# The penalty of each score as a 17th lane of the query-key products, laid by ScalarE, in a windowed attention on one core

## The reference

```python
q = _ln(silu(x @ Wq).reshape(B, L, H, D), q_g, q_b)      # H = 16 heads of D = 16
k = _ln(silu(x @ Wkv)[..., :C].reshape(B, L, H, D), ...)
wp = silu(x @ Wwin + bwin)
width = sigmoid(wp[..., :H]) * 8 + 0.5
sharp = sigmoid(wp[..., H:]) * 9.5 + 0.5
rel = abs(arange(17) - 8)
scores = stack([einsum('blhd,blhd->blh', q, k_pad[:, w:w+L]) for w in range(17)]) * D ** -0.5
soft_mask = sigmoid((width[..., None] - rel) * sharp[..., None])
attn = softmax(scores - (1.0 - soft_mask) * 1e4, axis=-1)
out = sum(attn[..., w] * v_pad[:, w:w+L] for w in range(17))
x1 = layernorm(x + silu(out @ Wout))
```

## Time and profile before

| | |
|---|---|
| median of 3 runs | 1184.05 us (1183.74 to 1184.78) |
| profiled execution | 1187.74 us, of which the span is 1185.5 us |
| mean granted TensorE clock | 0.927 of full |
| busy share of the span | PE 81%, DVE 70%, ACT 39%, POOL 60% |
| first stage | about 0 to 110 us |
| window stage | about 110 to 500 us |
| cross attention and routing | about 505 to 730 us |
| experts, then the last norm | about 730 to 1145 us, then to the end |

### The profile page before, as it was taken

The page is one execution under the profiler, slowest core; times in us unless marked ns, Lnnn a source line. Parts: engine busy times, 40 slices in busy tenths (PEclk is TensorE's granted clock), DMA queues, the critical chain, the costliest instruction groups (busy, mean ns, idle before and its releaser), DMA issues.

```text
span 1185.5 us, 25126 instructions
## 1 busy us (share of the span) xinstructions
PE 960.9 (81%) x8135; PEld 774.8 (65%) x8136; DVE 825.9 (70%) x1264; ACT 461.7 (39%) x1055; POOL 712.9 (60%) x464
## 2 busy tenths in 40 slices
PE   7983089998989989678788249999999999999940
PEld 4541088888879979656566237777777777777720
DVE  4899999999999998138888764444444444444425
ACT  3676224444444444325656223222222222222215
POOL 3575599999999999200000055666666666666522
PEclk9998589999999999879999569999999999999985
DMA  3262012112211221478674402222222222222236
GB/s 102 72 120 54 22 41 67 53 58 67 66 56 54 67 66 45 168 256 273 193 236 160 164 28 37 47 41 47 42 46 41 45 44 44 44 45 44 27 80 226
DMA packets 70136, 100.46 MB, mean 85 GB/s; under 512 B 9312, under 2 KB 51872, under 8 KB 69152
## 3 DMA queue, kind: packets, MB, share of 16 engines
q1 hardware_dynamic: 52816, 76.86, 20.8%
q0 software_dynamic: 16128, 18.93, 10.1%
q10 hardware_dynamic: 1152, 4.19, 0.9%
HBM read 73.96 MB, written 26.38 MB: 85 GB/s over the span
## 4 chain that ended last, share of the span: by engine, by line
PE 44%; DVE 28%; issue 15%; DMA 5%; POOL 3%; ACT 3%; DVEq 0%; SPq 0%; ACTq 0%; POOLq 0%
PE psum L757 16%; DVE mid L1392 11%; PE psum L765 10%; PE psum L767 5%; PE psum L616 3%; PE psum L685 2%; DMA sum_dram<-arena,mid 2%; DVE psum L1399 2%; PE psum L596 2%; DVE arena L1529 1%; PE psum L749 1%; PE psum L659 1%; ACT arena L1082 1%; PE psum L599 1%; DMA out<-arena 1%
## 5 line engine op out<-in xcount | busy, mean ns | idle before, releaser
L616 PE MATMUL psum<-consts,mid 128*128 128x128 f32 x2176 | 255.5, 279 | 58.4 <-POOL mid L1155 58.4
L616 PEld LDWEIGHTS psum<-consts,mid 128*128 128x128 f32 x2176 | 251.9, 195 | 66.6 <-issue 48.2
L757 PE MATMUL psum<-arena 128*128 128x128 f16 x3456 | 291.2, 221 | 4.6 <-issue 2.7
L757 PEld LDWEIGHTS psum<-arena 128*128 x3456 | 243.4, 98 | 76.2 <-issue 9.5
L1155 POOL TENSOR_TENSOR mid<-arena 128x2304 f32<-128x2304 f32 (+1 forms) x62 | 251.1, 4072 | 10.0 <-POOL arena L1146 7.0
L765 PE MATMUL psum<-arena 128*128 x576 | 218.1, 380 | 5.3 <-DVE arena L1681 1.2
L1233 POOL DMA_INDIRECT sum_dram<-arena,mid x72 | 142.0, 1972 | 46.5 <-issue 24.3
L1690 DVE SCALAR_TENSOR_TENSOR arena<-psum,arena 128x256 f32<-128x256 f32 x72 | 34.8, 484 | 189.8 <-ACT arena L1054 121.4
L767 PE MATMUL psum<-arena 128*128 x576 | 157.0, 273 | 0.0
L1054 ACT ACTIVATE arena<-psum,arena 128x256 f32<-128x256 f32 x72 | 34.1, 473 | 301.5 <-PE psum L767 301.5
L1392 DVE TENSOR_TENSOR mid<-psum,arena 128x4352 f32<-128x4352 f32 x32 | 149.9, 4683 | 0.6 <-issue 0.4
(11 more groups left out here) (194 smaller groups left out, 1443.3 us busy)
## 6 DMA issues: line engine op xcount, KB each, us to landing
arena<-w_t SPq DMA_DIRECT2D x64, 256.0 KB, 2.8
arena<-w_t SPq DMA_DIRECT2D x16, 1024.0 KB, 10.4
arena<-x SPq DMA_DIRECT2D x32, 128.0 KB, 2.1
arena<-x_dram SPq DMA_DIRECT2D x8, 512.0 KB, 5.5
arena<-ctx_t SPq DMA_DIRECT2D x8, 512.0 KB, 6.4
arena<-ctx SPq DMA_DIRECT2D x8, 512.0 KB, 6.9
x_dram<-mid SPq DMA_DIRECT2D x8, 512.0 KB, 3.3
arena<-sum_dram SPq DMA_DIRECT2D x8, 512.0 KB, 4.9
```

Of the source, the lines that this page charges most:

```text
L616: last = nc.tensor.matmul(psum[:, u, c * P:(c + 1) * P], products[half][:, w, c * P:(c + 1) * P], ident, start=(a + w == 0 and c == 0), st ...
L757: last = nc.tensor.matmul(dst, block_of(w, e, 0, c * F + j * P, P), x[:, u, c * P:(c + 1) * P], start=(k == 0 and c == 0), stop=(k == 2 an ...
```

## The change

The products get a 17th lane: `qk_prod` becomes 17 places by 16 heads by 17 lanes. DVE's multiplication writes lanes 0 to 15. ACT writes lane 16 with the penalty, by two activations (Copy with a scale) that read `gate`: 144 and 128 elements, each written 17 elements apart. DVE's sum then reads 4624 elements and writes the penalised scores straight into `score`, in SBUF; `raw` and the two SCALAR_TENSOR_TENSOR instructions go. The sum waits for `penalties_laid`, and ACT lays the penalties of step t at the head of its `window(t)`, before it waits for `score_ready` of t. For t = 0 they are laid earlier, between the square root of the last heads and the second gates, and DVE's sum of step 0 comes after `last_gates`.

To make room, `reach` (no longer read) leaves the constants, and the 128x128 matrix of ones becomes one column read with stride 0 by the two matmuls that use it. The buffers that lay behind `qk_prod` start 272 elements later. ACT's loop is cut at step 24, where the place of `gate` wraps round.

```diff
+LANES = D + 1
+QK = K * H * LANES
...
-        mid = sb("mid", [P, 2 * K * E])
+        mid = sb("mid", [P, QK + K * E])
...
-        ones_pp = sb("ones_pp", [P, P])
+        ones_col = sb("ones_col", [P, 1])
+        ones_pp = ones_col[:, :].to_broadcast([P, P])
...
-        qk_prod = mid[:, 0:K * E]
+        qk_prod = carve(mid, 0, K, H, LANES)
...
@@ ScalarE
-            def window(t, u, i, more=True):
+            def lay_penalties(t, gate_at):
+
+                if past(t, 1):
+                    act.wait_ge(qk_summed, t)
+                gates = row(gate, t + gate_at).rearrange("p a h r -> p r (a h)")
+                lane = qk_prod[:, :, :, D]
+                nc.scalar.activation(lane[:, R:, :], gates, ACT.Copy, scale=-PENALTY / SCALE).then_inc(penalties_laid, 1)
+                nc.scalar.activation(lane[:, R - 1::-1, :], gates[:, 1:, :], ACT.Copy,
+                                     scale=-PENALTY / SCALE).then_inc(penalties_laid, 1)
+
+            def window(t, u, i, gate_at, more=True):
+                if not isinstance(t, int) or t:
+                    lay_penalties(t, gate_at)
                 act.wait_ge(score_ready, t + 1)
                 nc.scalar.activation(score[:, u, :], score[:, u, :], ACT.Exp, scale=SCALE).then_inc(exp_done, 1)
...
             head_roots(GROUPS - 1)
+            act.wait_ge(gate_done, 1)
+            lay_penalties(0, GROUP)
             gates(1)
...
@@ VectorE
+            def sum_products(t, u):
+
+                dve.wait_ge(qk_multiplied, t + 1)
+                dve.wait_ge(penalties_laid, 2 * t + 2)
+                if past(t, 2):
+                    dve.wait_ge(prob_made, t - 1)
+                nc.vector.tensor_reduce(score[:, u, :].rearrange("p (h w) -> p w h", w=K), qk_prod, op=ALU.add,
+                                        axis=AX.X).then_inc(qk_summed, 1)
...
-                nc.vector.tensor_tensor(qk_prod[:, :].rearrange("p (w c) -> p w c", c=E), queries,
-                                        k_all[:, bass.ds(t, K), :], ALU.mult).then_inc(qk_multiplied, 1)
+                nc.vector.tensor_tensor(qk_prod[:, :, :, 0:D], queries.rearrange("p w (h d) -> p w h d", d=D),
+                                        k_all[:, bass.ds(t, K), :].rearrange("p w (h d) -> p w h d", d=D),
+                                        ALU.mult).then_inc(qk_multiplied, 1)
                 if isinstance(t, int) and t == 0:
                     last_heads()
                 if past(t, 1):
                     sum_up(t - 1, 1 - u)
-                dve.wait_ge(qk_multiplied, t + 1)
-                nc.vector.tensor_reduce(raw.rearrange("p (h w) -> p w h", w=K),
-                                        qk_prod[:, :].rearrange("p (w h d) -> p w h d", h=H, d=D), op=ALU.add, axis=AX.X).then_inc(qk_summed, 1)
+                if not (isinstance(t, int) and t == 0):
+                    sum_products(t, u)
                 if past(t, 1):
                     invert(t - 1, 1 - u)
                 if isinstance(t, int) and t == 0:
                     last_gates()
-                    dve.wait_ge(gate_done, 1)
+                    sum_products(0, 0)
...
-                nc.vector.scalar_tensor_tensor(by_head[:, :, R:], gates, -PENALTY / SCALE, raw_by_head[:, :, R:],
-                                               ALU.mult, ALU.add).then_inc(penalised, 1)
-                nc.vector.scalar_tensor_tensor(by_head[:, :, R - 1::-1], gates[:, :, 1:], -PENALTY / SCALE,
-                                               raw_by_head[:, :, R - 1::-1], ALU.mult, ALU.add).then_inc(penalised, 1)
-                dve.wait_ge(penalised, 2 * t + 2)
```

More of the change, by code:

```diff
@@ L46 @@
 MASKED = 1e10
-LOW = 10856
+LOW = 10824
 N_EXP, TOP, F = 8, 2, 1024
@@ L59 @@
 AT_IDENT = 0
-AT_REACH = AT_IDENT + P
-AT_MASK = AT_REACH + K
+AT_MASK = AT_IDENT + P
 AT_BELOW = AT_MASK + P
@@ L76, in host_consts @@
         i == j,
-        wide(np.abs(np.arange(K) - R)),
         np.where(j > i, -MASKED, 0.0),
@@ L171, in decoder_layer @@
         ident = consts[:, AT_IDENT:AT_IDENT + P]
-        reach = consts[:, AT_REACH:AT_REACH + K]
-        ones_pp = sb("ones_pp", [P, P])
+        ones_col = sb("ones_col", [P, 1])
+        ones_pp = ones_col[:, :].to_broadcast([P, P])
         minus_half = sb("minus_half", [P, 2 * H])
@@ L249, in decoder_layer @@
         w_exp = carve(mid, scale_at + 8, 2).bitcast(I32)
-        assert scale_at + 10 <= 2 * K * E
+        assert scale_at + 10 <= QK + K * E
         gate_col = next_low("experts", 4, 1)
@@ L272, in decoder_layer @@
         v_all = carve(big, (CHUNK + ROWS) * E, ROWS, E)
-        qk_prod = mid[:, 0:K * E]
-        av_prod = [carve(mid, K * E, W0, E), carve(mid, (K + W0) * E, K - W0, E)]
+        qk_prod = carve(mid, 0, K, H, LANES)
+        av_prod = [carve(mid, QK, W0, E), carve(mid, QK + W0 * E, K - W0, E)]
         av_last = [carve(mid, 0, W0, E), carve(mid, W0 * E, K - W0, E)]
         x_step = carve(mid, 0, 2, X_QUAD, C, P)
[L278 to L281, removed]
+        act_qk = carve(mid, QK, 2, 2 * E)
+        cen_qk = carve(mid, QK + 4 * E, 2, 2 * E)
+        sq_qk = carve(mid, QK + 8 * E, 2, 2 * E)
+        head_r = carve(mid, QK + 12 * E, GROUP, 2 * H)
         gate = next_low("window", CHUNK, H, R + 1)
@@ L388, in decoder_layer @@
         qk_summed = sem("qk_summed")
-        penalised = sem("penalised")
+        penalties_laid = sem("penalties_laid")
         q_beside = sem("q_beside")
@@ L643, in _ @@
             pe.wait_ge(w_summed, 1)
-            nc.tensor.matmul(psum[:, 0, 0:2], ones_pp[:, :], w_sum[:, :], start=True, stop=True).then_inc(w_total, 1)
+            nc.tensor.matmul(psum[:, 0, 0:2], ones_pp, w_sum[:, :], start=True, stop=True).then_inc(w_total, 1)
             def transpose_x1(u, c):
@@ L725, in _ @@
                              picked.rearrange("p t n -> p (t n)"), start=True, stop=True)
-            nc.tensor.matmul(psum[:, 1, 0:TILES * N_EXP], ones_pp[:, :],
+            nc.tensor.matmul(psum[:, 1, 0:TILES * N_EXP], ones_pp,
                              picked.rearrange("p t n -> p (t n)"), start=True, stop=True).then_inc(counted, 1)
@@ L937, in _, with windows @@
             head_roots(GROUPS - 1)
+            act.wait_ge(gate_done, 1)
+            lay_penalties(0, GROUP)
             gates(1)
-            steps(act, LAG, window, LAG)
-            steps(act, CHUNK - 2, window, LAG, LAG)
+            def windows(a, z):
+                turn = CHUNK - GROUP
+                for z_part, gate_at in ((min(z, turn), GROUP), (z, GROUP - CHUNK)):
+                    if a < z_part:
+                        steps(act, z_part, lambda t, u, i: window(t, u, i, gate_at), LAG, a)
+                        a = z_part
+            act.wait_ge(gate_done, 2)
+            windows(0, LAG)
+            windows(LAG, CHUNK - 2)
             for t in range(CHUNK - 2, CHUNK):
-                window(t, t % 2, t // 2, more=False)
+                window(t, t % 2, t // 2, GROUP - CHUNK, more=False)
             for t in range(CHUNK - LAG, PARTS[2][1]):
@@ L1097, in _ @@
             nc.gpsimd.memset(v_all[:, R + CHUNK:ROWS, :], 0.0).then_inc(halo_zeroed, 1)
-            nc.gpsimd.memset(ones_pp[:, :], 1.0).then_inc(fills_made, 1)
+            nc.gpsimd.memset(ones_col[:, :], 1.0).then_inc(fills_made, 1)
             nc.gpsimd.memset(minus_half[:, :], -0.5).then_inc(fills_made, 1)
@@ L1386, in last_gates, with window @@
                     gate_args(1, r)
-            def window(t, u, i, gate_at):
+            def sum_products(t, u):
[5 more added lines that the diff above has]
+                                        axis=AX.X).then_inc(qk_summed, 1)
+            def window(t, u, i):
                 dve.wait_ge(q_beside, t + 1)
                 queries = q_psum[:, u:u + 1, :].to_broadcast([P, K, E])
-                nc.vector.tensor_tensor(qk_prod[:, :].rearrange("p (w c) -> p w c", c=E), queries,
-                                        k_all[:, bass.ds(t, K), :], ALU.mult).then_inc(qk_multiplied, 1)
+                nc.vector.tensor_tensor(qk_prod[:, :, :, 0:D], queries.rearrange("p w (h d) -> p w h d", d=D),
+                                        k_all[:, bass.ds(t, K), :].rearrange("p w (h d) -> p w h d", d=D),
+                                        ALU.mult).then_inc(qk_multiplied, 1)
                 if isinstance(t, int) and t == 0:
@@ L1404, in window @@
                     last_gates()
-                    dve.wait_ge(gate_done, 1)
+                    sum_products(0, 0)
                 if isinstance(t, int) and 1 <= t <= K_PIECES:
                     scale_keys(GROUPS - 1, t - 1)
-                by_head = score[:, u, :].rearrange("p (h w) -> p h w", w=K)
-                raw_by_head = raw.rearrange("p (h w) -> p h w", w=K)
-                gates = row(gate, t + gate_at).rearrange("p a h r -> p (a h) r")
                 dve.wait_ge(qk_summed, t + 1)
-                if past(t, 2):
-                    dve.wait_ge(prob_made, t - 1)
```

(9 more changed lines are left out.)

## The result

| | before | after |
|---|---|---|
| median | 1183.89 us (4 runs, 1181.8 to 1184.78) | 1378.97 us (4 runs, 1373.34 to 1381.02) |
| ratio | | 1.1643, 95% interval 1.1604 to 1.1682 |
| span of the profiled execution | 1185.5 us | 1378.3 us |

The account below looks back on a forecast made before the run. DVE bounds the window stage now, at 10.67 us a step; after the change a ring of waits gives 17.27 us for 28 steps, +186.5 us in total, so 1370 us, with an 8-in-10 range of 1322 to 1390.

Parts of the forecast that it names:

- The order makes a ring: Window stage: DVE's sum waits for penalties behind ACT's previous step, closing a loop of 15.94 us a step at full clock.
- Rival 3: Window stage: penalties are there when DVE is ready, only instruction count decides; 8 us less, 1176 us; chance 0.02.
- The transfer is in the ring: Window stage: ACT's squares wait for a weight piece held behind PE's L636; L861 to squares takes 6.98 us.
- Rival 2: Window stage: weight piece there in time, squares don't wait; 13.24 us a step, 1258 us; chance 0.04.
- The clock: Window stage: PE idles about 4 us ahead of L625, falls to 1.2 GHz, adding 1.60 us to a step that pays.
- S(3): Start of POOL's subtraction of step 3 in the window stage, put at 171.3 us.
- S(31): Start of POOL's subtraction of step 31 in the window stage, put at 655.4 us against 465.92 before.
- five of six: Share of window steps taken to pay for PE's low clock: 1.33 us a step, giving 17.27.
- Rival 1: Window stage: PE's clock stays up, 15.94 us a step; 1333 us; chance 0.19.
- The terms: Parts of one window step, from DVE's sum to the next: 15.94 us at full clock, 17.54 with every step low.
- A mis-sized term: ACT's two added penalty activations in each window step, taken as 0.30 us each, plus 0.1 for the signal to DVE.
- Start and end: First window steps, setting the third step's subtraction at 171.3 us, and the stage's end, taken as -3 us (0 to -5).

Follow-up runs that it names:

- kernel 1: Changed kernel with ACT laying the penalties of the next step right behind the query copy: 1178.34 us, ratio 0.9947 to the kernel before.
- kernel 10: Kernel before the change, plus one wait: DVE's sum of step t waits for ACT's squares of t-1; no lane, no ACT penalties: 1371.98 us, ratio 1.1582.
- kernel 6: kernel 1 with POOL multiplying for the silu of step t-3 while it waits for its own probabilities: 1175.71 us, ratio 0.9929.
- 7: Kernel before the change with the same move of POOL's silu multiplication as kernel 6: 1184.13 us, ratio 0.9999.
- kernel 3: Changed kernel with SP starting weight piece t ahead of the x row of step t-1 instead of behind it: 1265.64 us, ratio 1.0676.
- kernel 4: Changed kernel with 15 more unused 128x128 matmuls a step while PE waits for ACT's copy: 1343.16 us, ratio 1.1332.
- kernel 5: Changed kernel with the edits of kernel 3 and kernel 4 together, 15 added matmuls a step: 1286.03 us, ratio 1.0861.

## Why the prediction was right, step by step

- *The order makes a ring.* Right, and it is the whole loss: kernel 1 undoes it by place alone, kernel 10 makes it by one wait alone. Rival 3, the gain of 8 us, was about the value of the instructions (8.4 us, kernel 6 against 7) and wrong only by the place.
- *The transfer is in the ring.* Right: kernel 3. SP's waits for L636 grew to 434.5 us in 27 times, 16.1 us each, against 9.4 in the earlier trace rows. Rival 2 (1258 us, at the full clock) is close to what kernel 3 makes (1266).
- *The clock.* Right in kind, too low in number: of the 28 turns from S(3) to S(31) 27 paid, 1.54 us a turn in the mean where five of six gave 1.33, and from the third step of the stage on none escaped. The section "HAM oscillation — how this bites in real kernels" of the page "TensorE: Matmul & The Clock Gate" of the Trainium skill, which the prediction names, says that in such a loop every burst starts at the low clock; from the third step on the trace agrees. The reason given for five of six, idle times longer than the 2.13 us ahead of one fall, doesn't carry: 3.23 us of idle at 173.14 left the full clock, and 3.24 us at the same place in kernel 3 didn't. The idle just ahead of a product doesn't decide alone. Rival 1 (1333 us) is about what kernel 4 makes (1343, with one step at the low clock and eight held by the added matmuls).
- *The terms.* Predicted at the low clock 17.54 us, measured 17.68 in the step above: sum to peak 5.05 (5.13), peak to subtraction 0.47 (0.52), to the exponential 0.68 (0.75), to L861 0.65 (0.62), to the squares 8.69 (8.58), squares 1.24 (1.24), penalties and signal 0.90 (0.70). The mean over 28 steps is (662.00 - 171.40) / 28 = 17.52. The prediction's sum at the full clock with the share that was measured gives 15.94 + 1.54 = 17.48, so most of the quarter of a microsecond by which 17.27 falls short is the share of the clock, 1.54 against 1.33.
- *A mis-sized term* is the penalties, 0.83 us with the signal in the mean of these steps and 0.70 taken: two activations of 144 and 128 elements took 0.45 and 0.42 us, though the 272 elements of the exponential took 0.43 in one. The terms from the sum to the exponential were put too high by 0.04 to 0.07 us each, which cancels it; that is luck.
- *Start and end.* S(3) was put at 171.3 and came at 171.40, with S(1) and S(2) each about 0.6 us later than put (144.9 and 154.3; 145.46 and 154.95), so this too hit closer than its parts. The end gave 193.7 - 196.1 = -2.4 us, -3 was taken. That L900 would start "a little over 8 us after S" left out the prediction's own low clock; with it the terms give 9.95, and the row (L912) is at 322.12 - 312.10 = 10.02.
- *The remainder.* The loss by the medians is 195.1 us, 8.6 above the 186.5 forecast. S(31) is 6.6 later than put (662.0 against 655.4), the end 0.6, the stages behind it give back 0.9 (192.8 by the spans, 193.7 at L649). The last 2.3 stand between spans and medians: the profiled execution of the kernel before was itself above its median.

## What to carry to other kernels

Before work goes to an engine that is idle more than half of the time, look at where in its queue it lands: an in-order queue makes the new work as late as everything ahead of it, and a consumer that needs it closes a ring through all that the queue waits for, other engines and transfers included. Write the ring out start to start from one step of the timeline; here that gave the new time to 1%, with the low clock of an engine that the ring makes wait as one of its terms. Then look for the earliest place at which the inputs are there, often one step ahead: the same two instructions cost 195 us in one place and gained 6 in another.

## What the runs showed of the hardware that was not expected

- Two ScalarE copies of 144 and 128 elements, read 9 elements apart and written 17 apart, took 0.45 and 0.42 us; 256 elements side by side took 0.36 to 0.42. Whether the gap of the reads or of the writes costs it wasn't separated.
- VectorE's sum over groups of 17 ran at the rate of the one over groups of 16 (4.97 us for 4624 elements, 4.68 for 4352; the first writes to SBUF, the second to PSUM), and products written with a gap after each 16 took the same 4.68 us as without.
- Work without a use made the kernel faster: 15 matmuls more a step held TensorE's clock and took 36 us off (kernel 4), and cost 20 where the wait that they filled had become shorter (kernel 5 against kernel 3).
- The length of TensorE's idle time just ahead of a product did not alone tell its clock: 2.13 us led to 1.2 GHz in the kernel before, 3.24 in kernel 3, while 3.23 in the changed kernel and 2.76 in kernel 3 (L630 at 332.29) left 2.4 GHz.
